# Graph network stack: normalizations and rank weights on ScalarE, rank sums on TensorE

## The reference

```python
def _layernorm(x, axis=-1, eps=1e-5):
    m = jnp.mean(x, axis=axis, keepdims=True)
    v = jnp.var(x, axis=axis, keepdims=True)
    return (x - m) / jnp.sqrt(v + eps)
```

```python
agg = 0.25*quantile(0.25) + 0.5*quantile(0.5) + 0.25*quantile(0.75)
out = x + agg
y = (relu(out @ W1 + b1) @ W2 + b2) * mask
```

## Time and profile before

| | |
|---|---|
| median of three executions | 2798.1 us (2797.18 to 2803.76) |
| the profiled execution's own time | 2827.46 us |
| its span, first to last instruction | 2825.7 us |
| mean granted TensorE clock | 0.701 |
| busy: PE, DVE, POOL, ACT | 54%, 58%, 46%, 16% of the span |

### The profile page before, as it was taken

How to read it: one execution, slowest core, us unless ns; L and a number is a source line. 1 busy time by engine, 2 the same in 40 slices (tenths; PEclk the granted TensorE clock), 3 DMA queues, 4 the chain that set the end, 5 groups by cost and what they waited for, 6 DMA issues and landing times.

```text
span 2825.7 us, 24253 instructions
## 1 busy us (share of the span) xinstructions
PE 1535.0 (54%) x8885; PEld 858.3 (30%) x8997; DVE 1625.1 (58%) x2443; ACT 462.6 (16%) x756; POOL 1299.3 (46%) x1196
## 2 busy tenths in 40 slices
PE   3735637556374655638366464836636375565232
PEld 2412414323142332314233241423314243233111
DVE  2511827649285574928467383755828376494926
ACT  3101212102021120202112020210302121020000
POOL 1072370735527173552717447172643707265550
PEclk9766658667586766759577676866768586777555
DMA  3122130313213131321313123131322313112120
GB/s 99 54 25 53 46 55 21 75 11 86 19 40 62 24 75 12 83 22 34 67 20 77 15 53 54 29 69 8 88 18 50 55 22 75 10 23 20 23 24 4
DMA packets 106610, 120.13 MB, mean 43 GB/s; under 512 B 71486, under 2 KB 71614, under 8 KB 106430
## 3 DMA queue, kind: packets, MB, share of 16 engines
q0 software_dynamic: 36864, 37.82, 14.2%
q1 hardware_dynamic: 69566, 79.98, 9.2%
HBM read 109.27 MB, written 8.45 MB: 42 GB/s over the span
## 4 chain that ended last, share of the span: by engine, by line
DVE 40%; PE 24%; issue 18%; another core or an unknown queue 15%; ACT 2%; DVEq 1%; POOL 0%; DMA 0%; POOLq 0%; ACTq 0%; SPq 0%
PE ps_tr L596 7%; DVE lists L1181 4%; DVE slots L1001 4%; PE ps_tr L604 4%; DVE slots L1000 3%; PE ps_prod L615 3%; PE ps_tr L585 2%; PE ps_misc L775 2%; DVE slots L1008 2%; DVE slots L1009 2%; DVE xc L977 1%; DVE stat L979 1%; DVE stat L976 1%; PE ps_misc L704 1%
## 5 line engine op out<-in xcount | busy, mean ns | idle before, releaser
L403 POOL DMA_INDIRECT slots<-h_rows,row_no x1152 | 1287.4, 1118 | 1433.2 <-DVEq L1187 1087.0
L596 PE MATMUL ps_tr<-adj_t,y_mid 128*128 128x512 bf16 x960 | 301.7, 459 | 223.7 <-issue 121.3
L1223 DVE TENSOR_TENSOR y_mid<-ps_prod,scales 128x512 f32<-128x512 f32 x48 | 33.2, 692 | 554.2 <-remote 407.5
L448 ACT ACTIVATE columns_t<-ps_tr 128x512 f32<-128x512 f32 (+1 forms) x192 | 113.0, 595 | 1409.2 <-PE ps_tr L604 888.7
L596 PEld LDWEIGHTS ps_tr<-adj_t,y_mid 128*128 128x128 bf16 x1024 | 105.6, 112 | 471.1 <-issue 416.0
L1181 DVE MAX8 lists<-ps_key 128x8 f16<-128x1024 f32 x128 | 157.8, 1233 | 112.8 <-PE ps_key L685 69.4
L585 PE MATMUL ps_tr<-h_t,w_l_sb 65*128 65x512 f32 x192 | 151.3, 896 | 107.6 <-issue 76.1
L695 PE MATMUL ps_misc<-parts_w,select_t 128*128 128x64 bf16 x384 | 36.7, 220 | 268.1 <-issue 229.3
L472 ACT ACTIVATE adj_n<-adj_f 128x1024 f16<-128x1024 f32 x128 | 134.3, 1050 | 229.1 <-remote 80.7
L604 PE MATMUL ps_tr<-adj_t,low 128*64 128x512 bf16 x1024 | 157.9, 419 | 16.9 <-issue 16.6
L615 PE MATMUL ps_prod<-both_ident,columns_t 128*128 128x64 f32 x768 | 107.9, 297 | 101.6 <-issue 91.6
(11 more groups left out here) (210 smaller groups left out, 2539.2 us busy)
## 6 DMA issues: line engine op xcount, KB each, us to landing
adj_f<-in_adj SPq DMA_DIRECT2D x128, 512.0 KB
slots<-h_rows,row_no POOLq DMA_INDIRECT x1152
x<-in_x SPq DMA_DIRECT2D x16, 256.0 KB
h_rows<-h SPq DMA_DIRECT2D x16, 256.0 KB, 2.9
out<-x SPq DMA_DIRECT2D x16, 256.0 KB
xc<-in_L_gnn_W SPq DMA_DIRECT2D x1, 64.0 KB
w_sb<-in_L_gnn_W SPq DMA_DIRECT2D x2, 32.0 KB
h_rows<-zeros SPq DMA_DIRECT2D x2, 32.0 KB, 1.5
```

The lines of the kernel that those rows point to most:

```text
L403: pool.indirect_dma_start(out=slots[:, slot_of(par, s), t * C:(t + 1) * C], out_offset=None, in_=table[par][:, :], in_offset=bass.Indirect ...
L448: act.activation(dst, view, ACT.Copy, scale=scale).then_inc(tr_free, 1)
L596: nc.tensor.matmul(dst[:, :], top_halves(pair_of)[:, j, :], adj_t[g % 3][:, columns[j]], start=(j == 0 and not begun), stop=False)
```

## The change

ACT takes over the squares, their sums and the final scaling of all four norms, and the weighting of the ranks, tile by tile, since its scale and bias are one value for a partition. PE adds up the seven weighted ranks, the node's own row (`h2`) and the wide rows directly in turned form (features on partitions), so that the eight transposes of `agg` and the 24 products of `spread_wide` are gone; the 13 wide ranks are summed by 13 f32 products with the identity. DVE keeps the means, reciprocals and the splitting of sums. `degrees` and norm0's mean move behind the `propagate` of "v1", `add_mlp` moves ahead of the row lists, norm0's squares move ahead of v3, and `mlp_rows` ahead of the row keys on PE. POOL's gather waits for PE's sums instead of DVE's.

`RANKS` holds seven (slot, rank) pairs and `wide_ranks` 13 ranks. The diff, cut to its core:

```diff
@@ gather (POOL), own_rows (ACT)
-                    pool.wait_ge(slots_read, g - 1)
+                    pool.wait_ge(tr_full, TR["agg.1", g - 2] + 1)
@@ ACT
-            def deviation(name, g):
-                act.wait_ge(var_ready, NORM[name, g] + 1)
-                act.activation(s_std, s_var, ACT.Sqrt, bias=eps_col[:, :], scale=1.0 / C).then_inc(std_ready, 1)
+            def norm_spread(name, g):
+                _, less_mean, var, std, _, _ = stat_of(name)
+                act.wait_ge(mean_ready, NORM[name, g] + 1)
+                for t in range(T):
+                    last = act.activation(square[:, t * C:(t + 1) * C], x[g % 4][:, t * C:(t + 1) * C], ACT.Square,
+                                          bias=less_mean[:, t:t + 1], accum_out=var[:, t:t + 1])
+                last.then_inc(squared, 1)
+                act.wait_ge(squared, NORM[name, g] + 1)
+                act.activation(std, var, ACT.Sqrt, bias=eps_col[:, :], scale=1.0 / C).then_inc(std_ready, 1)
+
+            def norm_apply(name, g, to, ready):
+                _, _, _, _, rstd, shift = stat_of(name)
+                act.wait_ge(rstd_ready, APPLY[name, g] + 1)
+                for t in range(T):
+                    last = act.activation(to[:, t, :], x[g % 4][:, t * C:(t + 1) * C], ACT.Relu,
+                                          bias=shift[:, t:t + 1], scale=rstd[:, t:t + 1])
+                last.then_inc(ready, 1)
+
+            def weigh(g, first, last):
+                act.wait_ge(sorted_ready, g + 1)
+                for t in range(first, last):
+                    for s, wire in RANKS:
+                        value = slots[:, slot_of(par, s), t * C:(t + 1) * C]
+                        done = act.activation(value, value, ACT.Copy, scale=weight[par][:, t, wire:wire + 1])
+                    done.then_inc(weighed, 1)
+
+            def weigh_wide(g):
+                act.wait_ge(merged_ready, g + 1)
+                for r in wide_ranks(par):
+                    done = act.activation(merged[:, r, :], merged[:, r, :], ACT.Copy, scale=w[:, r:r + 1])
+                done.then_inc(wide_weighed, 1)
@@ ACT's turn
                 casts(0, 1)
-                    deviation("norm1", b)
+                    norm_spread("norm1", b)
+                    from_tr("select", b, ...)
                 casts(1, 2)
-                    from_tr("select", b, ...)
+                    norm_apply("norm1", b, h_rows[:, :, 0:C], h1_ready)
                     halves("h1", b, h1_t[:, :])
-                casts(2, 6)
+                casts(2, 5)
+                    weigh(c, 0, 4)
                     half_of("v1", b, 0, columns_t[:, :])
-                casts(6, 7)
+                    weigh(c, 4, 6)
                     half_of("v1", b, 1, columns_t[:, :])
-                casts(7, 8)
+                    weigh_wide(c)
+                    weigh(c, 6, 8)
+                casts(5, 8)
                     degree_roots(n)
                     halves("v2", b, columns_t[:, :])
+                    norm_spread("norm0", n)
                     halves("agg", c, columns_t[0:C, :])
...
-                    deviation("norm3", c)
-                    deviation("norm2", b)
-                    half_of("h3", c, 0, columns_t[:, :])
+                    norm_spread("norm3", c)
+                    norm_spread("norm2", b)
+                    norm_apply("norm3", c, z, z_ready)
+                    norm_apply("norm2", b, tiles(h2[b % 2]), h2_ready)
                     own_rows(b)
-                    half_of("h3", c, 1, columns_t[:, :])
-                    deviation("norm0", n)
+                    norm_apply("norm0", n, y, y_ready)
+                    halves("h3", c, columns_t[:, :])
@@ PE
-            def spread_wide(g):
...
+            def sum_wide(g):
+                pe.wait_ge(wide_weighed, g + 1)
+                misc_turn("wide", g)
+                for r in ranks_of:
+                    last = nc.tensor.matmul(ps_misc[:, 0:C], ident_f[:, :], merged[:, r, :],
+                                            start=(r == ranks_of[0]), stop=(r == ranks_of[-1]))
+                last.then_inc(misc_full, 1)
+
+            def turned_sums(g):
+                pe.wait_ge(wide_summed, g + 1)
+                for i in range(2):
+                    tr_turn(f"agg.{i}", g)
+                    for t in range(i * (T // 2), (i + 1) * (T // 2)):
+                        pe.wait_ge(weighed, g * T + t + 1)
+                        dst = tr_bank(f"agg.{i}", g)[0:C, t % (T // 2) * P:(t % (T // 2) + 1) * P]
+                        nc.tensor.matmul(dst, h2[par][:, t * C:(t + 1) * C], ident_f[:, :], start=True, stop=False)
+                        for k in range(3):
+                            nc.tensor.matmul(dst, parts_w[:, k, :], select_t[g % 3][:, t * P:(t + 1) * P],
+                                             start=False, stop=False)
+                        for s, wire in RANKS:
+                            last = nc.tensor.matmul(dst, slots[:, slot_of(par, s), t * C:(t + 1) * C], ident_f[:, :],
+                                                    start=False, stop=(wire == SLOTS - 1))
+                    last.then_inc(tr_full, 1)
@@ PE's turn
                     turned_back("v1", "v1", b, both_ident, False)
-                    spread_wide(c)
                     own_weights("v2", b, DEPTH - 2)
+                    sum_wide(c)
                     (v2's halves, loop_rows, turned_back)
-                    transpose_features("agg", c, lambda t: agg[:, t, :], C)
+                    turned_sums(c)
                     own_weights("v3", b, DEPTH - 3)
                     (hidden_rows and v3's halves, loop_rows)
+                    mlp_rows(c)
                     row_keys(b, 0)
                     turned_back("v3", "v3", b, both_ident, False)
                     row_keys(b, 1)
                     cross_drops(b)
                     row_keys(b, 2)
                     count_over(b)
-                    mlp_rows(c)
@@ DVE: norm_stats, norm_apply, wide_sum, narrow_weighing, narrow_sum, aggregate are replaced by
+            def norm_begin(name, g):
+                step(v.tensor_reduce(total, tiles(x[g % 4]), AX.X, ALU.add))
+                step(v.tensor_scalar(less_mean, total, -1.0 / C, None, ALU.mult))
+                dve.sem_inc(mean_ready, 1)
+            def norm_scale(name, g, scale_by=None):
+                dve.wait_ge(std_ready, NORM[name, g] + 1)
+                step(v.reciprocal(rstd, std))
+                if scale_by is not None:
+                    step(v.tensor_tensor(rstd, rstd, scale_by, ALU.mult))
+                step(v.tensor_tensor(shift, less_mean, rstd, ALU.mult))
+                dve.sem_inc(rstd_ready, 1)
+            def wide_parts(g):
+                (waits for misc_full of "wide", then the four small steps that make parts_w out of PSUM)
@@ DVE's turn
                     merge_rest(c)
-                    wide_sum(c)
-                    degrees(n)
                     propagate(b, "v1")
-                    narrow_weighing(c)
-                    narrow_sum(c)
-                    aggregate(c)
+                    degrees(n)
+                    norm_begin("norm0", n)
+                    wide_parts(c)
                     propagate(b, "v2")
                     widest(...), wide_drops(b)
+                    add_mlp(c)
+                    norm_begin("norm3", c)
                 row_lists(0, 2)
                     layer1_out(b)
+                    norm_begin("norm2", b)
                     wide_lists(b)
+                    norm_scale("norm3", c)
                 row_lists(2, 3)
                     flag_crowds(b)
-                    add_mlp(c), norm_stats(x[c % 4], z)
+                    norm_scale("norm2", b)
                 row_lists(3, 4)
-                    norm_apply("norm3", c, z)
+                    dve.wait_ge(z_ready, c + 1)
                     split(z_mid, low_z)
-                (norm_stats and norm_apply of norm2 and norm0, between row lists 4 to 7)
+                    norm_scale("norm0", n, d0[n % 2])
+                row_lists(4, 8)
+                    row_numbers(b)
+                    dve.wait_ge(y_ready, n + 1)
                     split(y_mid, low)
```

149 lines of the change are left out of this document (56 added, 93 removed).

## The result

The kernel after took 3030.72 us (median of 4 runs, 3027.86 to 3035.93), the kernel before beside it 2800.93 us (4 runs, 2797.18 to 2816.76): ratio 1.0811, 95% interval 1.0766 to 1.0856. The forecast was 2983 us, with a range of 2850 to 3120. The profiled execution took 3030.36 us with a span of 3028.6; the sum had given 3012 for it. So the sum over the profile was short by 18 us; the other 29 us of the miss are the profiled execution of before standing above its own median, which that of after doesn't do.

A forecast was written before the change was run, and what follows sets the result against it. Bound by an order of work, not an engine. Per turn +8.5 (tail) + 2 (ACT) - 1 (DVE) = +9.5, +133 us in 14 turns, +185 with the ends: 3012 us profiled, 2983 us as median, range 2850 to 3120.

The forecast's parts named there:

- the sum: Whole kernel: +9.5 us a turn, +133 in 14 turns, +185 with the ends and first batches; 3012 us profiled.
- the blocked stretch: 50.6 us in the examined turn; PE's completions reach others late until the last gathers land; work within it is free.
- the first stretch: First 54.7 us of a turn, up to v1: -1 us for DVE, +2 for ACT's weighings, ends 0 and +9.
- v2: Third stretch, 13.1 us: removing DVE's 9 us of weighting, adding and `aggregate` beside PE's products is worth nothing.
- The sums on PE: Ahead of v3: 16.7 us of products replace transposes taking 1.28; everything after on PE starts 15.4 us later.
- Rival B: Cheap sums on PE, each product at a transpose's 0.13 us: 7 us x 14 less, 2885 us; chance 0.13.
- Rival C: Sums on PE at half the clock: +16.7 us x 14, 3217 us; chance 0.05.
- The tail after it: From v2's `propagate` to the row numbers: 55.4 us against 46.9, +8.5 us a turn.
- cover gone: In the tail: DVE's savings remove cover for layer 3's halves on PE, which become late; no size of its own.
- the end: Last two batches, without row lists to hide behind: batch 14 +30 us (0 to +36), batch 15 +17.
- rival D: The block breaks, v1 and v2 pass, sums run under the gather: 2512 us, or up to no change; chance 0.14.
- A: Block earlier or ACT's queue late: front +9 us a turn instead of +2, 3100 us; chance 0.21.

The follow-up runs named there:

- one_weighed: Kernel after with six of seven narrow-rank weighings on ACT left out, PE's sums whole: 2162.55 us, ratio to before 1.0341.
- sums_only: Kernel before with weighing on ACT and sums on PE, norms and DVE's order unchanged: 2481.51 us, ratio 1.1831.
- norms_only: Kernel after with the rank sums done as before, keeping norms on ACT and the new order: 2028.91 us, ratio to before 0.9673.
- the other base: Kernels before and after, unedited, run again in later executions without the blocked stretch: 2094 and 2205 us, ratio 1.0517.
- after_again: Kernel after, unedited, run again in later executions without the blocked stretch: 2204.72 us, ratio to before 1.0517.
- before_again: Kernel before, unedited, run again in later executions without the blocked stretch: 2090.7 us, median 2094.15 in seven runs beside it.

## Why the prediction was right, and where it was off

**What bounds the kernel.** An order of work, not an engine: right. Each step moved the time by what it moved on the cycle of tail and front, not by what it moved in busy time: 21.6 us a batch less on DVE came out as a loss. That what falls into the blocked stretch is free held nearly, where there was one: in the turns of batches 1 to 13 v2's `propagate` came after the landing in 12 of 13 before and in all after, and the front moved by 3.0 us. But I took the stretch for a property of the kernel. It belonged to the executions profiled, and 47 us of a 167 us turn hung on it.

**In the first stretch.** Worth -1 for DVE, +2 for ACT's queue, ends 0 and +9. Measured together +3.0 with the block and +0.5 without. The ACT part by itself is 2.7 us (`one_weighed`, for 48 of 56 operations), so the +2 was nearly right in size, though I had worked it out for casts and weighings behind the block and it stands without one. The 28 weighings that I put at 7 us took 6.8. What I had not weighed is the root behind them: in `sums_only` it costs 12 us a turn (the front falls from 83.6 to 71.5 with `degrees` moved). The change avoided that cost by its order, and I had put `degrees` down as something that "fits", without naming what its wait would hold up.

**v2.** Worth nothing: consistent. `norms_only` keeps the 9 us of weighting, adding and `aggregate` on DVE and has v2's `propagate` at 68.6 us, the kernel after without them, but with the weighings on ACT, at 70.0. With most weighings left out too it is 67.3, 1.3 less; what the removal by itself is worth no run tells.

**The sums on PE.** 16.7 us forecast, 15.5 measured, 0.22 us a product where I took 0.24. v3's own weights start 15.4 us after v2's `propagate`, where I had named 18. Rival B's price, that of a transpose, would have been 0.13: it falls. Rival C, half clock, falls too: the granted clock from 1138.0 to 1153.5 us, the sums' own time, is 1.00, and 0.94 over the whole tail (the last of these four, cut at the block's begin, its end and the end of v2):

```profile
1019.90:1072.00 52.10, 37.27 (x234) 21.61 (x232) 45.12 (x58) 30.75 (x84) 42.76 (x31) 0.74 0.36 81
1072.00:1129.00 57.00, 19.52 (x64) 10.25 (x63) 3.75 (x11) 12.67 (x44) 39.15 (x41) 0.55 0.31 33
1129.00:1141.00 12.00, 11.26 (x64) 6.75 (x65) 3.40 (x8) 4.14 (x19) 0.00 (x0) 0.74 0.01 1
1141.00:1193.80 52.80, 46.22 (x355) 31.59 (x354) 27.52 (x59) 19.63 (x67) 0.03 (x1) 0.94 0.08 26
```

**The tail after it.** 46.9 to 55.4 us forecast, +8.5; measured 48.6 to 54.6 as means of 13 turns, +6.0 (and 48.9 to 55.1, +6.2, on the other base). The new tail was right to 1 us. The old one was read from a single turn, whose 46.9 is short of the mean by 1.7: two thirds of the error are that choice. DVE's idle ahead of `add_mlp` was put at 18 us and is 17.1. PE's 15.4 us do eat DVE's saving: without the block DVE works 9.5 us less in the tail (38.73 to 29.26) and is idle 15.7 more (10.17 to 25.87), which makes the +6.2. That layer 3's halves become late is so, but small: DVE waits for the keys of rows 6 and 7 behind them, 0.7 and 2.5 us in the turn shown above, 0.3 together before. That is 3 us of the 9.5:

```profile
1187.33 1.23 DVE L1223 MAX8 lists<-ps_key 128x8 f16<-128x1024 f32 x1 [0.70 <-PE ps_key L738]
...
1191.08 1.23 DVE L1223 MAX8 lists<-ps_key 128x8 f16<-128x1024 f32 x1 [2.52 <-PE ps_key L738]
```

And "what DVE gains here is cover gone" would have the norms worth less once the sums are there. The runs show the opposite: the sums by themselves cost 13.5 us of tail, the norms with their order save 3.7 without the sums and 7.2 with them, and both together cost 6.2 and not 9.8.

**The sum.** +9.5 a turn forecast, +8.9 measured: 8 us too much over 13 turns, and 4 too much at the start. The turn's total is closer than its parts: the front came out at +3.0 where I had +1 and the tail at +6.0 where I had +8.5, so that part of it is luck. The mis-sized term is the end. From batch 14's gather to batch 15's I had one ordinary +9.5; it was +31.5. From there to the end I had +47; it was +54.8. Together the end was 30 us short. On the other base the same two are +8.8 (115.46 to 124.22) and +15.2 (188.4 to 203.6), so the block makes both. In the kernel before it came late in batch 15's turn, 80 us after the gather's start, with v2 already done. In the kernel after it came at 50 us, ahead of v1: DVE waited there for v1 for 51.2 us, until 100.9, and again, for the wide sum, until 110.2. In the last turn the wide sum and PE's sums stood in it (a wait of 38.2 us and the one of 51.5 in the table of waits). I had named this lateness as the ground of rival D, and had not asked what it would cost if the one early turn fell back into line with the others.

**Rivals.** A (ACT's queue late, +9 in the front) did not come: the front grew by 3.0 us with the block and by 0.5 without. The Trainium skill (ScalarE: Activation LUTs, Rules for kernel authors) advises mul, add and relu on VectorE. On busy time the runs agree: 896 weighings of 335 ns, 223.0 us, on ACT against 64.5 us of the earlier trace rows for the same products on DVE. On the kernel's time they agree for the weighings, as far as the runs go: DVE did them beside v2's products, and on ACT 48 of them cost 2.6 us a batch. They don't for the norms, which with their new order make the kernel 3% faster on ACT. D (the block breaks, faster) did not come: in the first profile v2's release stayed behind the landing in every turn. Without any block v2's `propagate` stands at 70.0 us, as D wanted it, but in the kernel before it does too (69.5), and then the change is slower by 5.2%. That sums under the gather would be free is not so either: they did run under it (the tail of `after_again` has 26.5 us of POOL), and cost the same 6 us, since it is PE's order and not the gather that they stand in.

## What to carry to other kernels

To offload an engine that is 58% busy, look for what the receiving engine holds up in its own queue, not for how idle it is: here PE's 15 us stood ahead of the one product that everyone waited for, and ACT's weighings cost little except where a small root was queued behind them and DVE's next step behind that. Split such a change before judging it: the norms with their order gained 3%, the sums with `degrees` moved lost 11%, and the whole hid a gain worth keeping. And where a tail and the next front are one cycle, work moved out of the tail isn't gone; measure the whole turn.

## What the runs showed of the hardware that I had not expected

The same program took 2797 to 2827 us in the first five executions and 2083 to 2124 us in 29 later ones on four chips, and the kernel after 3031 and 2205 us. Nearly the whole difference is a stretch of up to 50 us in each turn, in which PE issues one instruction every 1.4 us, or 2.8 for a weight load and its product, and others see its completions late. It ends about when the gather's last rows land. One profile of each kernel shows it; the other seven of the first executions are known by their time alone. PE's timeline in the kernel after, in that stretch:

```profile
1118.43 0.58 PE L657 MATMUL ps_tr<-adj_t,low 128*64 128x512 bf16 x1 [2.21 <-issue]
1121.23 0.58 PE L657 MATMUL ps_tr<-adj_t,low 128*64 128x512 bf16 x1 [2.21 <-issue]
1124.03 0.58 PE L657 MATMUL ps_tr<-adj_t,low 128*64 128x512 bf16 x1 [2.21 <-issue]
```

Without it eight such products take 1.05 us, as the line of L604 in `before_again` shows, and the same 72 gathers stream beside them. The clock isn't it: the granted clock is 0.55 there, but the product itself takes 0.58 us, and it is 2.2 us of waiting that come with it. So the gathers may be a condition, since the stretch ends about where they do, but they are not the cause by themselves. What differs between the two groups of executions stays open. It could not be tried, since none of the later executions showed the stretch.
